# Four stages of the first attention, one turn later in every engine's order

## The chip, the cores and the metric

One core of a Trainium2 chip runs the whole program. Its five engines (TensorE, VectorE, ScalarE, GpSimd and SyncE, in the profile PE, DVE, ACT, POOL and SP) each work through a queue of instructions in order, and wait for one another by semaphores. The metric is the device time of one execution in microseconds, as the median of several runs.

## What is computed

The reference is a block of two layers over `x`, 32 batches of 128 rows and 128 features, with a context of 77 keys per batch. Cut to what matters:

```
x = x + tanh(g_xattn[0]) * attention_0(layernorm(x), ctx)     # one head, masked softmax, layernorm of its result
x = x + tanh(g_ffn[0])   * ffn_0(layernorm(x))                # best of 8 experts by a router, plus a shared expert
x = x + tanh(g_xattn[1]) * attention_1(layernorm(x), ctx)     # 16 heads, relative bias
x = x + tanh(g_ffn[1])   * ffn_1(layernorm(x))                # best of 8 maps by a signature
```

Only the first line and the routing of the second concern the change. The router needs, for each row of the normalised `x`, eight logits (`x_ @ router.T`), the expert of the largest, and then a place for the row among all rows of that expert.

## The kernel before

**The first attention** (`attend_0`) works on pairs of batches, 0 to 15. For a pair, the steps run through four engines:

- TensorE transposes the rows (`rows_T`, L494), multiplies context by weights (`keys`, L509 to L516, and `values`, L502), makes the scores (`scores`, L525), transposes the probabilities (`probs_T`, L533) and weighs the values (`weigh`, L541).
- VectorE makes the bias of the mask (`mask_bias`, L713), the masked scores and their maximum (`masked`, L745, L749), the values with their bias (`values_0`, L723), the statistics of the result (`attend_stats`, L758 to L764), and the new rows with their statistics (`centred` L772, `residual` L784 to L795).
- GpSimd turns variances into factors (`inv_std0`, L892 to L894; `inv_std1`, L902 to L905).
- ScalarE copies results out of PSUM (`keys`, `rows_T`, `probs_T`, `values_1` L641), takes the exponentials (`exps`, L649) and writes the normalised rows `XN` (`norm1`, L660).

**The four stages that the title means** come behind these. TensorE transposes the normalised rows of a pair (`norm1_T`, L549), ScalarE copies the transpose into `XNT` (`norm1_T`, L667), TensorE multiplies it by the router (`logits`, L569). Four pairs make a quarter. When the last pair of a quarter (3, 7, 11, 15) has its logits, VectorE picks the experts and counts them (`route`, L805 to L816), TensorE adds up ranks (`ranks`, L554 and L555), and VectorE turns them into slots (`slots`, L823 to L827). GpSimd then scatters the rows of a batch to their slots in memory (`scatter`, L848): twelve batches within the loop, twenty behind it.

**The order** is written out by hand, for each engine apart. `written_out` takes a list of stages with a lag each; in turn t it issues, in the order of the list, stage by stage, the item t minus its lag (lags count from the smallest in the list). So a stage with a larger lag stands in a later turn, behind the younger pairs' other work. An engine's queue is in order: an instruction that waits holds back all that stand behind it.

Some waits name other pairs than their own, because two stages share a bank of PSUM. `norm1_T` on TensorE (L547) waits until ScalarE has copied the rows' transposes that were issued before it; `norm1_T` on ScalarE (L666) waits for TensorE in the same way; `ranks` (L560) and `scores` (L521) keep the ranks and the scores of one bank apart.

Near the end of the stage, where less work is left per turn, the table also issues filler matmuls (`warm`, L590), whose results nobody reads: in front of the transposes of pairs 14 and 15, behind `weigh` of pair 15, and in front of the logits of pairs 13 to 15.

**What follows.** TensorE ends the stage with the counts (L603) and the ranks of the last quarter. Then the shared expert runs over all rows (`hidden`, L993 and L994; `down`, L1004), while GpSimd issues the remaining scatters. When all scatters have landed and a table of experts is ready, SyncE loads sorted tiles of 128 rows (`xs`, L970), and TensorE transposes them (L1024) and runs the experts. The second attention (`attend_1`) and the second feed-forward take the rest of the program.

Of the kernel before, what the change touches and what calls it, by code (L numbers as in the profile page):

```python
# [47 lines left out]
PAIR = 2  # L48
NG = B // PAIR
QB = 8  # L50
# [85 lines left out]
def wait(eng, sem, value):  # L136

    if isinstance(value, int) and value <= 0:
        return
    eng.wait_ge(sem, value)  # L140
# [27 lines left out]
def written_out(n, stages):  # L168

    first = min(lag for _, lag in stages)  # L170
    for turn in range(n + max(lag for _, lag in stages) - first):
        for stage, lag in stages:
            item = turn - (lag - first)
            if 0 <= item < n:
                stage(item)
# [200 lines left out]
def attend_0(nc, sb, sem, sems, bank, a, m, f, units):  # L376
# [18 lines left out]
    xT = [halves(units["hT"][0][u], 0) for u in two]  # L395
    sm = [sb(f"sm{u}", [128, PAIR, SK]) for u in two]
# [25 lines left out]
    s = sems("a", "w0 cen pe0 act0 stat var rs q xT xTs v v0 v1 mkr mk mb sc sm mx ex pT pTs u umv "  # L422
                  "iv inv z zg xmv inv1 xn1 xT2 xT2s lg sh cum rk wh slot")
# [54 lines left out]
    def pe_program(pe):  # L478
# [39 lines left out]

        def scores(g):
            wait(pe, s["sm"], g)  # L520
            wait(pe, s["wh"], 2 * ((g - 11) // (QB // PAIR)) + 1)  # L521
            pe.wait_ge(s["xTs"], g + 1)
            pe.wait_ge(s["mk"], g + 1)
            for b in range(PAIR):
                last = nc.tensor.matmul(bSC[:, b * SK:(b + 1) * SK], xT[g % 2][:, b, :], M[g % 2][:, b * SK:(b + 1) * SK],  # L525
                                        start=True, stop=True)
            last.then_inc(s["sc"], 1)
# [16 lines left out]
        def norm1_T(g):  # L544
            pe.wait_ge(s["xn1"], g + 1)
            wait(pe, s["xT2s"], g)
            pe.wait_ge(s["xTs"], min(g + 6, NG))  # L547
            for b in range(PAIR):
                last = nc.tensor.transpose(bT2[:, b * 128:b * 128 + 128], XN[:, PAIR * g + b, 0:D], ident)  # L549
            last.then_inc(s["xT2"], 1)  # L550

        def ranked(q):
            pe.wait_ge(s["cum"], q + 1)
            nc.tensor.matmul(place(q), ones[:, :], upto[q % 2][:, :, 1:QB + 1], start=True, stop=False)  # L554
            nc.tensor.matmul(place(q), tri, QH[q % 2][:, :, 1:QB + 1], start=False, stop=True).then_inc(s["rk"], 1)  # L555

        def ranks(g):
            q, i = divmod(g, QB // PAIR)
            if i == QB // PAIR - 1 and q < NQ - 1:
                wait(pe, s["sm"], min(g + 7, NG))  # L560
                if q == NQ - 2:
                    pe.wait_ge(s["mk"], NG)
                ranked(q)
# [23 lines left out]
        def warm(n):  # L587
            pe.wait_ge(s["v1"], NG)
            for k in range(n):
                nc.tensor.matmul(bV[:, 0:3 * PK], identb[:, :], mb[0][:, :, :].rearrange("p (o b) k -> p o (b k)", o=1)  # L590
                                 .to_broadcast([128, 3, PK]), start=True, stop=True)

        def before(table):
            def stage(g):
                if g in table:
                    warm(table[g])
            return stage

        written_out(NG, [(before({14: 7, 15: 3}), 7), (norm1_T, 7), (rows_T, 1), (values, 3), (weigh, 4), (before({15: 6}), 4),
                         (keys, 0), (probs_T, 3), (ranks, 8), (scores, 1), (before({13: 2, 14: 2, 15: 2}), 7), (logits, 7), (unit, 18)])  # L600
        warm(8)
        pe.wait_ge(s["cum"], NQ)
        nc.tensor.matmul(bLG[:, 0:E], ones[:, :], upto[(NQ - 1) % 2][:, :, QB], start=True, stop=True).then_inc(f["s_count"], 1)  # L603
# [2 lines left out]
    def act_program(act):  # L606
# [56 lines left out]

        def norm1_T(g):
            act.wait_ge(s["xT2"], g + 1)
            act.wait_ge(s["xT"], min(g + 7, NG))  # L666
            nc.scalar.activation(XNT[:, pair(g), :], bT2[:, 0:PAIR * S].rearrange("p (b s) -> p b s", b=PAIR),  # L667
                                 ACT.Copy).then_inc(s["xT2s"], 1)

        def unit(j):  # L670
            if j < EARLY:
                for k in range(HC):
                    units["silu"](act, j, k)

        written_out(NG, [(unit, 19), (values_1, 3), (norm1, 6), (probs_T, 3), (keys, 0), (exps, 2), (rows_T, 0), (norm1_T, 6)])

    def dve_program(dve):
        nc.vector.memset(ones[:, :], 1.0).then_inc(s["cen"], 1)
# [158 lines left out]
            if 0 < j <= EARLY:  # L837
                units["add"](dve, j - 1)

        written_out(NG, [(route, 10), (values_0, 5), (attend_stats, 6), (shifted, 5), (centred, 6), (residual, 7), (masked, 3), (slots, 10), (mask_bias, 0), (unit, 20)])  # L840
        dve.wait_ge(s["act0"], 6)
        nc.vector.tensor_scalar(qscale[:, :], qscale[:, :], 4.0, HD ** -0.5, ALU.min, ALU.mult).then_inc(s["cen"], 1)
        dve.wait_ge(s["cen"], 6)
# [904 lines left out]
```

## Time and profile before

| what | value |
|---|---|
| median of 3 runs | 523.37 us (522.79, 523.37, 527.62) |
| the profiled execution | 525.38 us |
| its span, first to last instruction | 523.6 us |
| mean granted clock of TensorE | 0.965 of full speed |
| first attention, shared expert, experts, second layer | to about 108, 140, 222 and 523.6 us |

The profile is of one execution. A line such as L549 is a line of the kernel. In a timeline a row can stand for several instructions of one form that follow each other, and `[0.45 <-ACT XN L660]` says that the engine sat idle for 0.45 us in front of it, until that instruction of ScalarE had ended. Transposes and products of TensorE in this data type are each recorded as two matmuls, so a pair's two transposes are a row of four, two of which overlap their neighbours. "PEclk" is the clock of TensorE that was granted, as a share of its full speed. Times of single rows are of this one execution.

### The profile page before, as it was taken

What the parts mean: (1) busy time and instruction counts of PE and PEld (TensorE: products, weight loads), DVE (VectorE), ACT (ScalarE), POOL (GpSimd) and SP (SyncE); (2) the same over time, 40 slices, a digit from 0 to 9 for tenths busy, and PEclk for the clock granted to TensorE, in tenths of its full rate; (3) what the DMA queues carried; (4) which work ended last, traced back from release to release, by engine and by line L of the source; (5) the groups of instructions that cost most, each with busy time, mean ns of one, the idle gap of its engine ahead of it and who ended that gap; (6) DMA issues with size and microseconds to landing.
All of it is one profiled execution on the core that took longest, in us unless ns stands there. A gap on an engine that the chain in (4) does not pass through costs nothing.

```text
span 523.6 us, 12435 instructions
## 1 busy us (share of the span) xinstructions
PE 482.2 (92%) x3408; PEld 303.7 (58%) x3408; DVE 386.9 (74%) x1178; ACT 300.5 (57%) x981; POOL 346.6 (66%) x813
## 2 busy tenths in 40 slices
PE   6977888799999999879999999999999999999993
PEld 5967776455655666655555555555555555555441
DVE  2879998667333334345899999999999999999852
ACT  3746665322254555266776776676766767776630
POOL 5554777777244555462778787888878787878532
PEclk9979897899999999987999999999999999999997
DMA  8885350022144322100000000000000000000000
GB/s 233 161 113 157 92 160 12 16 77 62 45 106 120 82 74 68 47 11 7 11 13 22 21 12 21 13 21 11 22 13 21 16 19 21 13 17 10 7 6 16
DMA packets 33924, 25.77 MB, mean 49 GB/s; under 512 B 8105, under 2 KB 31281, under 8 KB 33825
## 3 DMA queue, kind: packets, MB, share of 16 engines
q1 hardware_dynamic: 30864, 19.48, 15.3%
q0 software_dynamic: 2272, 4.67, 2.8%
q10 hardware_dynamic: 720, 0.83, 0.6%
q8 instruction: 29, 0.48, 0.4%
q14 instruction: 39, 0.31, 0.2%
HBM read 16.89 MB, written 8.39 MB: 48 GB/s over the span
## 4 chain that ended last, share of the span: by engine, by line
PE 48%; DVE 2%; issue 1%; POOL 1%; POOLq 0%; ACT 0%; DVEq 0%
PE bank L1376 13%; PE bank L1325 8%; PE bank L1311 8%; PE bank L1301 6%; PE bank L1392 2%; PE bank L1362 2%; PE bank L1297 2%; PE bank L1358 1%; PE bank L1342 1%; PE bank L1346 1%; PE bank L1337 1%; PE bank L1287 1%; PE bank L1381 1%; PE bank L1283 1%; PE bank L1398 1%
## 5 line engine op out<-in xcount | busy, mean ns | idle before, releaser
L1439 ACT ACTIVATE wgu<-wgu,top 128x77 f32<-128x77 f32 x256 | 67.4, 347 | 15.7 <-DVE top L1541 15.7
L1376 PE MATMUL bank<-w,xn3T 128*128 128x512 f32 x128 | 71.7, 644 | 0.1
L1449 ACT ACTIVATE PRT<-bank 128x512 f32<-128x512 f32 (+1 forms) x128 | 54.5, 426 | 29.0 <-PE bank L1311 28.5
L983 POOL DMA_INDIRECT routed<-ys,to x39 | 37.4, 960 | 43.7 <-DVE ys L1186 35.0
L1311 PE MATMUL bank<-cst,wgu 128*128 128x128 f32 x320 | 60.2, 286 | 1.6 <-ACT wgu L1439 1.3
L1531 DVE TENSOR_TENSOR wgu<-bank,biasQ 128x616 f32<-128x616 f32 x64 | 50.9, 795 | 7.0 <-PE bank L1301 5.6
L1325 PE MATMUL bank<-PRT,VP 128*32 128x128 f32 x1024 | 55.0, 287 | 0.7 <-ACT PRT L1449 0.7
L1541 DVE TENSOR_REDUCE top<-wgu 128x8 f32<-128x616 f32 x64 | 50.2, 784 | 1.1
L1301 PE MATMUL bank<-KB,QT 32*128 32x308 f32 x256 | 50.2, 433 | 0.0
L1181 DVE TENSOR_TENSOR hid<-actg,bank 128x256 f32<-128x256 f32 x39 | 16.4, 421 | 41.8 <-ACT actg L1090 41.8
L1311 PEld LDWEIGHTS bank<-cst,wgu 128*128 128x128 f32 x320 | 37.7, 142 | 16.1 <-issue 13.2
L1677 POOL TENSOR_TENSOR wgu<-V 128x256 f32<-128x256 f32 x32 | 37.9, 1183 | 6.5 <-DVE V L1602 6.5
L1039 PE MATMUL bank<-wgu,xsT 128*128 x78 | 40.9, 605 | 0.0
L848 POOL DMA_INDIRECT sorted_x<-XN,slot x32 | 33.8, 1056 | 8.5 <-issue 8.5
L1637 POOL TENSOR_TENSOR VP<-XN,cst 128x64 f32<-128x64 f32 x128 | 34.9, 305 | 0.0
L1325 PEld LDWEIGHTS bank<-PRT,VP 128*32 128x32 f32 x1024 | 20.2, 108 | 25.2 <-issue 19.7
L1656 POOL TENSOR_TENSOR x2b<-x,rows 128x128 f32<-128x128 f32 x32 | 14.6, 455 | 27.7 <-DVE x L1569 27.7
L1548 DVE TENSOR_TENSOR wgu<-wgu,top 128x616 f32<-128x616 f32 x32 | 27.1, 846 | 0.0
L1432 ACT ACTIVATE QT<-bank,qbias,qscale 128x128 f32<-128x128 f32 x32 | 14.6, 456 | 21.7 <-PE bank L1287 21.7
L1376 PEld LDWEIGHTS bank<-w,xn3T 128*128 128x128 f32 x128 | 19.1, 188 | 13.4 <-ACT OHT L1482 6.9
L1055 PE MATMUL bank<-wdn,hidT 128*128 x156 | 25.8, 288 | 1.1 <-ACT hidT L1095 1.1
L1090 ACT ACTIVATE actg<-bank 128x256 f32<-128x256 f32 x39 | 15.0, 385 | 19.8 <-PE bank L1039 19.8
(232 smaller groups left out, 1261.6 us busy)
## 6 DMA issues: line engine op xcount, KB each, us to landing
xs<-sorted_x SPq DMA_DIRECT2D x39, 64.5 KB, 1.8
wgu<-in_wgu SPq DMA_DIRECT2D x4, 512.0 KB
y<-routed SPq DMA_DIRECT2D x32, 64.0 KB, 1.8
out<-res SPq DMA_DIRECT2D x32, 64.0 KB, 1.7
ctxT<-in_ctxT SPq DMA_DIRECT2D x16, 77.0 KB, 3.0
mask<-in_mask SPq DMA_DIRECT2D x16, 77.0 KB, 3.8
wdn<-in_wdn SPq DMA_DIRECT2D x2, 512.0 KB
X<-in_x SPq DMA_DIRECT2D x1, 768.0 KB, 5.5
```

Source lines behind the costliest of these rows:

```text
L983: nc.gpsimd.indirect_dma_start(routed, bass.IndirectOffsetOnAxis(ap=to[:, t:t + 1], axis=0), ys[t % WAYS][:, :], None).then_inc(st_y[t % W ...
L1039: nc.tensor.matmul(bH[t % 2][:, :], xsT[t % 2][:, :], wgu[:, bass.ds(experts[t], 1), :], start=True, stop=True).then_inc(e["h"], 1)
L1301: nc.tensor.matmul(bS[i][:, 0:HG * SK], QT[u][rows, :], KB[u][rows, :, :], start=False, stop=True).then_inc(s["sc"], 1)
L1311: last = nc.tensor.transpose(bP[end][:, i * 128:i * 128 + 128], SB[u][:, c, :], ident)
L1325: last = nc.tensor.matmul(bO[32 * j:32 * j + 32, half * S:half * S + S], VP[u][:, half, j, end, :, :].rearrange("p t r -> p (t r)"), PT[ha ...
L1376: nc.tensor.matmul(map_bank(b, k)[:, :], xn3T[u][:, :], w2[:, k * HT:(k + 1) * HT, :], start=True, stop=True).then_inc(s["f"], 1)
L1439: last = nc.scalar.activation(SC[u][:, head, :], SC[u][:, head, :], ACT.Exp, bias=top[u][:, head:head + 1])
L1449: nc.scalar.activation(PT[half][:, k], bP[end][:, 0:k.stop - k.start], ACT.Exp if half else ACT.Copy).then_inc(s["pTs"], 1)
L1531: nc.vector.tensor_tensor(half(SC[u][:, k, :]), bSS.rearrange("p c (h k) -> p c h k", h=HG), half(biasQ[:, k, :]), ALU.add).then_inc(s["sb ...
L1541: nc.vector.tensor_reduce(top[u][:, k], SC[u][:, k, :], AX.X, ALU.max, negate=(h == 0)).then_inc(s["mx" if h else "lo"], 1)
L1637: last = nc.gpsimd.tensor_tensor(VP[u][:, c, :, end, :, 0:HD], VF[:, first:first + HG, bass.ds(b, 1), :].to_broadcast([128, HG, 2, HD]), o ...
L1677: nc.gpsimd.tensor_tensor(sum2[u][:, :, :], picked[u][:, 0:2, :], picked[u][:, 2:4, :], ALU.add).then_inc(s["s2"], 1)
```

## The change

In each engine's list the stages `norm1_T`, `logits`, `route`, `ranks` and `slots` get a lag larger by one: on TensorE `norm1_T` and `logits` 7 becomes 8 and `ranks` 8 becomes 9, with the two fillers' tables that belong to them; on ScalarE `norm1_T` 6 becomes 7; on VectorE `route` and `slots` 10 becomes 11. The waits that count the other pairs between are set to match. `norm1` (L660), GpSimd's and SyncE's lists and all other stages stay. No instruction is added or removed.

```diff
         def scores(g):
             wait(pe, s["sm"], g)
-            wait(pe, s["wh"], 2 * ((g - 11) // (QB // PAIR)) + 1)
+            wait(pe, s["wh"], 2 * ((g - 12) // (QB // PAIR)) + 1)
...
         def norm1_T(g):
             pe.wait_ge(s["xn1"], g + 1)
             wait(pe, s["xT2s"], g)
-            pe.wait_ge(s["xTs"], min(g + 6, NG))
+            pe.wait_ge(s["xTs"], min(g + 7, NG))
...
             if i == QB // PAIR - 1 and q < NQ - 1:
-                wait(pe, s["sm"], min(g + 7, NG))
+                wait(pe, s["sm"], min(g + 8, NG))
...
-        written_out(NG, [(before({14: 7, 15: 3}), 7), (norm1_T, 7), (rows_T, 1), (values, 3), (weigh, 4), (before({15: 6}), 4),
-                         (keys, 0), (probs_T, 3), (ranks, 8), (scores, 1), (before({13: 2, 14: 2, 15: 2}), 7), (logits, 7), (unit, 18)])
+        written_out(NG, [(before({14: 7, 15: 3}), 8), (norm1_T, 8), (rows_T, 1), (values, 3), (weigh, 4), (before({15: 6}), 4),
+                         (keys, 0), (probs_T, 3), (ranks, 9), (scores, 1), (before({13: 2, 14: 2, 15: 2}), 8), (logits, 8), (unit, 18)])
...
         def norm1_T(g):
             act.wait_ge(s["xT2"], g + 1)
-            act.wait_ge(s["xT"], min(g + 7, NG))
+            act.wait_ge(s["xT"], min(g + 8, NG))
...
-        written_out(NG, [(unit, 19), (values_1, 3), (norm1, 6), (probs_T, 3), (keys, 0), (exps, 2), (rows_T, 0), (norm1_T, 6)])
+        written_out(NG, [(unit, 19), (values_1, 3), (norm1, 6), (probs_T, 3), (keys, 0), (exps, 2), (rows_T, 0), (norm1_T, 7)])
...
-        written_out(NG, [(route, 10), (values_0, 5), (attend_stats, 6), (shifted, 5), (centred, 6), (residual, 7), (masked, 3), (slots, 10), (mask_bias, 0), (unit, 20)])
+        written_out(NG, [(route, 11), (values_0, 5), (attend_stats, 6), (shifted, 5), (centred, 6), (residual, 7), (masked, 3), (slots, 11), (mask_bias, 0), (unit, 20)])
```

In the three pieces below, rows without a sign stand in both kernels, rows with - only in the kernel before, rows with + only in the changed one.

ScalarE at the end of its list (`XN` is L660 of a pair, `XNT` the copy of a transpose, L667; the last pair's L660 is the second row):

```order
 L667 ACTIVATE XNT<-bank 128x256
 L660 ACTIVATE XN<-X,nb11,r11 128x128 x2
-L667 ACTIVATE XNT<-bank 128x256
+L667 ACTIVATE XNT<-bank 128x256 x2
 L1074 ACTIVATE wc<-wc 128x8
 L1080 ACT_TABLE_LOAD
```

Before, one copy followed the last L660; now two do, the copy of pair 14 among them.

VectorE behind the residual of pair 13 (L833 is a scaling of weights; the added rows are the statistics of pair 15 and the residual of pair 14; L805 and L806 begin the routing of pair 11):

```order
 L795 BN_AGGR mv<-st 128x2 x2
 L833 TENSOR_SCALAR wc<-wc,tg 128x256
+L758 BN_STATS st<-bank 128x6 x2
+L760 TENSOR_SCALAR es<-bank 128x2
+L764 BN_AGGR mv<-st 128x2 x2
+L772 SCALAR_TENSOR_TENSOR sg<-bank,mv,rows 128x128 x2
+L784 SCALAR_TENSOR_TENSOR X<-sg,ru,X 128x128 x2
+L790 BN_STATS st<-X 128x6 x2
+L795 BN_AGGR mv<-st 128x2 x2
 L805 TENSOR_REDUCE best<-bank 128x8
 L806 TENSOR_TENSOR cand<-bank,best 128x64
```

The routing of pair 11 now stands behind these seven steps; before, they followed it, with the slots of pair 11 between the residuals of pairs 14 and 15.

TensorE behind the weighing of pair 15 (L590 are fillers, L569 the logits of pair 11, L549 the transposes of pair 12, L554 and L555 the ranks of pair 11's quarter):

```order
 L541 MATMUL bank<-V,hT 128x129 x2
 L590 MATMUL bank<-mb,identb 128x462 x6
+L569 MATMUL bank<-wb,XNT 128x8 x2
+L549 MATMUL bank<-cst,XN 128x128 x2
 L554 MATMUL bank<-upto,ones 128x64
 L555 MATMUL bank<-QH,cst 128x64
```

Logits 11 and transposes 12 stood ahead of the weighing and now stand between the fillers and the ranks. What follows the ranks on TensorE (logits 12, transposes 13 and so on, with the fillers) stands in the same order as before.

## Rows read from the trace of the kernel before

**Rows 1.** Page of the profile, part 1: busy us (share of the span) xinstructions, whole span.
```profile
PE 482.2 (92%) x3408; PEld 303.7 (58%) x3408; DVE 386.9 (74%) x1178; ACT 300.5 (57%) x981; POOL 346.6 (66%) x813
```

**Rows 2.** Waits, 36.2 to 85.9 us: who waited for whom: us in total, times, longest us.
```profile
PE bank L549 <- ACT XN L660: 7.6, 8, 2.8
...
DVE mb L713 <- DMA mask<-in_mask: 3.0, 1, 3.0
...
DVE mv L795 <- issue: 0.2, 1, 0.2
```

**Rows 3.** Busy time of VectorE, 36.13 to 85.93 us: us of stretch, busy (instructions), clock, DMA.
```profile
36.13:85.93 49.80, 46.29 (x220) 0.95 0.40 117
```

**Rows 4.** Timeline, one turn: start us, us, engine line operation out<-in [idle before <-releaser].
```profile
40.43 0.23 DVE L713 TENSOR_SCALAR mb<-mask 128x154 bf16<-128x154 int32 x1
...
42.28 0.44 PE L549 MATMUL bank<-cst,XN 128*128 128x128 f32 x2 [0.45 <-ACT XN L660]
...
44.71 0.23 DVE L713 TENSOR_SCALAR mb<-mask 128x154 bf16<-128x154 int32 x1
```

**Rows 5.** Timeline of TensorE, 84 to 109 us.
```profile
87.78 0.69 PE L549 MATMUL bank<-cst,XN 128*128 128x128 f32 x2 [0.91 <-ACT XN L660]
...
96.21 0.41 PE L554 MATMUL bank<-upto,ones 128*128 128x64 f32 x2 [2.09 <-DVE upto L816]
...
98.86 2.78 PE L590 MATMUL bank<-mb,identb 128*128 128x462 bf16 x7
101.48 0.38 PE L549 MATMUL bank<-cst,XN 128*128 128x128 f32 x2
...
102.33 0.61 PE L569 MATMUL bank<-wb,XNT 128*128 128x8 f32 x4
102.80 0.75 PE L590 MATMUL bank<-mb,identb 128*128 128x462 bf16 x3
104.00 0.44 PE L549 MATMUL bank<-cst,XN 128*128 128x128 f32 x2 [0.46 <-ACT XN L660]
...
108.06 1.08 PE L993 MATMUL bank<-XNT,wc 128*128 128x512 f32 x2
```

**Rows 6.** Timeline of VectorE, GpSimd and ScalarE, 89 to 104 us.
```profile
90.21 0.42 DVE L723 TENSOR_TENSOR V<-bank,rows 77x256 f32<-77x256 f32 x1 [0.68 <-PE bank L502]
...
91.07 0.49 DVE L758 BATCH_NORM_STATS2 st<-bank 128x6 f32<-128x128 f32 x2 [0.44 <-PE bank L541]
...
94.36 0.22 DVE L805 TENSOR_REDUCE best<-bank 128x8 f32<-128x64 f32 x1
...
95.98 0.47 DVE L758 BATCH_NORM_STATS2 st<-bank 128x6 f32<-128x128 f32 x2
...
98.82 0.19 DVE L823 TENSOR_TENSOR where<-bank,QH 128x64 f32<-128x64 f32 x1
...
99.53 0.61 DVE L784 SCALAR_TENSOR_TENSOR X<-sg,ru,X 128x128 f32<-128x128 f32 x2
...
101.61 0.21 POOL L902 TENSOR_TENSOR ve<-mv,eps 128x2 f32<-128x2 f32 x1
...
103.07 0.88 ACT L660 ACTIVATE XN<-X,nb,r 128x128 f32<-128x128 f32 x2 [0.79 <-POOL nb L905]
```

**Rows 7.** Granted clock in stretches of the end: TensorE busy (instructions), PEclk, DMA, GB/s.
```profile
98.00:100.00 2.00, 2.00 (x8) 0.51 0.00 0
...
102.00:104.00 2.00, 1.47 (x9) 1.00 0.10 33
```

**Rows 8.** Timeline, 130 to 141 us: the start of the experts.
```profile
134.60 0.96 POOL L848 DMA_INDIRECT sorted_x<-XN,slot  x1 [0.31 <-issue]
...
137.71 2.58 SPq L970 DMA_DIRECT2D xs<-sorted_x  x3
...
140.64 0.33 PE L1024 MATMUL bank<-cst,xs 128*128 128x128 f32 x1 [0.33 <-DMA xs<-sorted_x]
```

**Rows 9.** Busy time, 108.06 to 140.2 us: PE, PEld, DVE, ACT, POOL, PEclk, DMA, GB/s.
```profile
108.06:140.20 32.14, 32.05 (x149) 20.13 (x148) 21.44 (x53) 7.17 (x12) 21.43 (x20) 1.00 0.24 65
```

## The prediction

> **What bounds the kernel now.** I read the page first, then the waits of the first attention, then one turn of the timeline, then its end engine by engine. The page shows TensorE busy for 92% of the span and VectorE for 74% [rows 1]; over the whole program TensorE is the engine to relieve. The stretch that the change touches is different, so the share of the span decides nothing here.
>
> In the waits of 36.2 to 85.9 us TensorE stands 7.6 us in front of L549, the transposes of the normalised rows, for ScalarE's L660 [rows 2]. That is the wait which the change addresses. The same view has only two entries for VectorE: one load of a mask, 3.0 us, which ends where the stretch begins (what TensorE lost or wins ahead of it is swallowed by that load), and 0.2 us without a releaser. VectorE waits for no other engine in these 50 us. It is busy for 46.29 of 49.80 us; the rest lies between instructions of its own chain [rows 3]. One turn shows the same: two L713 of neighbouring turns start 4.28 us apart, and inside that turn TensorE idles 0.45 us in front of L549 [rows 4]. So VectorE sets the turn from 36 to 86 us, and what TensorE waits there is slack.
>
> The end is another matter. At 90.21 and 91.07 VectorE does wait for TensorE, 0.68 and 0.44 us, for L502 and L541 [rows 6], which stand behind L549 at 87.78, itself 0.91 us late for L660 [rows 5]. From there a chain leads to the next stage: statistics of the last pair on VectorE, L902 and its followers on GpSimd (101.61), L660 on ScalarE (103.07), L549 (104.00), the logits L569 of that pair, the last routing on VectorE, and L993 at 108.06 [rows 5, 6]. From 108.06 TensorE works through the shared feed-forward without a gap, 32.05 of 32.14 us [rows 9]. Beside it GpSimd issues one scatter after another, the last at 134.60, the loads of sorted rows start at 137.71, and the second tile's transpose waits 0.33 us for its load at 140.64 [rows 8]. Two chains thus end within a microsecond of each other at 140: a gain in one alone is worth little.
>
> **The change part by part.** No instruction is added or removed and no DMA moves; GpSimd and SyncE keep their order. The summed durations stay; only positions in three queues count.
>
> *The turns from 36 to 86 us: 0.* TensorE's 7.6 us of waiting for L660 go, because the transposes of a pair stand a turn (4.28 us) behind it. What is late next is VectorE itself: L502 needs the bank that L723 and L641 free, and these follow VectorE's turn. The routing of pairs 3 and 7 and their slots come a turn later. By the rows of pair 11 that is 1.62 us (L805 at 94.36 to L758 at 95.98) and 0.71 us (L823 at 98.82 to L784 at 99.53) [rows 6]; they move within VectorE's continuous work and change no total. The scatters wait for the slots; the first is the only one near its limit, and GpSimd is busy with the statistics of that turn until about the time the slots are ready, so I add 0. Bounds: a gain of at most the 7.6 us if I misread VectorE, a loss of some 5 us if each of twelve turns lost as much as one L549 wait (0.45 us). I take 0, the row nearest being VectorE's own two entries.
>
> *The end on VectorE: a gain of 1.8 us.* L502 no longer waits behind L549, so the 0.68 and 0.44 us go: 1.12. The slots of pair 11 (0.71 us) now stand behind the residual of the last pair, not ahead of it. The routing of pair 11 moves from ahead of the statistics of pair 15 to behind the residual of pair 14, but it is still ahead of the last residual, so its 1.62 us neither come back nor are added. Together 1.8. GpSimd's own queue allows slightly less: between two statistics stands one scatter of about 1.3 us (0.96 and 0.31 in front of it at 134.60 [rows 8]), so I expect L902 of the last pair about 1.6 us earlier, near 100.0 instead of 101.61, and L660's pair ending near 102.3 instead of 103.95 (103.07 + 0.88).
>
> *The end on TensorE and ScalarE: a loss of 1.5 to 4.5 us on the same chain.* ScalarE's copy of a transpose (L667) now stands behind the L660 of the next pair. So the copy for pair 14 cannot start before L660 of pair 15 has ended, and on TensorE the logits of pair 14, three filler matmuls, and only then the transpose of pair 15 follow. Before, these lay in the time in which L660 of pair 15 was awaited: logits 14 at 102.33, fillers at 102.80, 0.75 long, and the transpose at 104.00 directly behind L660 [rows 5]. Now they stand behind it: copy 0.4 (the later half of the 0.85 us from transpose 14 at 101.48 to logits 14 at 102.33), logits 0.47 (102.33 to 102.80), fillers about 0.65 (0.75 with the last one's tail): 1.5 to 1.6 us at the full clock. From 102.3 this gives the transpose of pair 15 at 103.85, against 104.00: the gain of 1.6 is used up, net -0.1.
>
> The price at the lower clock is the open term. TensorE idles 2.09 us in front of L554 at 96.21, and between 98 and 100 us the granted clock is 0.51, its lower level of 1.2 GHz; there seven fillers take 2.78 us, 98.86 to 101.48 [rows 5, 7]. Three at 102.80, where the clock is full again (1.00 over 102 to 104), take 0.75, so seven would take about 1.5 there. In the changed order L554 waits for a routing that stands behind 2.84 us more of VectorE's work (L758 at 95.98 to L823 at 98.82), less the 1.1 gained before: 1.7 us later, and ahead of L554 TensorE now has logits 11 and transposes 12 as well, under 1 us. I estimate an idle time of 2.5 us or more. If the low level then covers logits 13 and the seven fillers, transpose 14 comes near 102.8 and that of pair 15 near 104.7: net +0.7. If it covers the whole end, every step doubles: logits and fillers 2.2 for 1.1, the seven fillers 2.6 for 1.5, transposes and the rank matmuls another 0.8: net +2.9. So the term lies between -0.1 and +2.9, and I take +0.7, the case nearest to the rows of before, where the low level covered 98 to 100 and was over by 102 [rows 7].
> The Trainium skill, page "TensorE: Matmul & The Clock Gate", Part 1 on the HAM clock gate, says that the throttled state is the default and that activity releases it, so an engine that has idled starts slow; it speaks against this change, because the idle time ahead of L554 grows. The rows at 96.21 and 98 to 100 us agree with it: idle, then the lower level. By the rule the sum is the +0.7 or the +2.9; by the full clock alone it would be -0.1.
>
> *The start of the experts: -0.3 us.* The scatters end about 1.6 us earlier, so the load for the second tile is there in time: the 0.33 us at 140.64 go [rows 8]. No more, since later loads wait for buffers that TensorE frees.
>
> **The sum.** 0 (turns) + 0.7 (end, net) - 0.3 (experts) = +0.4 us, against 525.38 us of the profiled execution (span 523.6, and 1.8 around it): 525.8. The median of the runs, 523.37, lies 2.0 below that execution; the same difference on it gives 523.8 us. About 1%, or 5.2 us, is what a measurement of this kernel can tell from no change.
>
> **The rivals.**
> A. *The end runs at the lower clock throughout*: +2.9 - 0.3, 526.0 us, slower. For it: the longer idle time in front of L554 and filler matmuls that stand on the path. Against it: in the rows of before the low level was over by 102. It decides from the point where transpose 14 comes after 103.
> B. *The gain of the end stays*: ScalarE's copy is early enough, and GpSimd's scatters set the start of the experts: -1.6 us, 521.8. For it: two chains of nearly equal length at 140. Against it: L667 of pair 14 stands behind L660 of pair 15 in ScalarE's queue, which is in order.
> C. *TensorE's wait was on the path*: the 7.6 us of the turns and the 0.91 and 0.46 us of the end come back, 9.0 us: 514.4 us. For it: TensorE's 92%. Against it: VectorE's two entries.
> D. *VectorE's turns get waits that they had not*: the transposes now follow the logits of an older pair, and if VectorE lost 0.45 us in each of twelve turns, +5.4: 529 us. For it: nothing in the rows but the tight order of ScalarE, in which L660 is not moved. Against it: TensorE gets slack, not work.
>
> **Chances.** The forecast 0.57 (522.3 to 525.3 by itself), A 0.20, B 0.12, C 0.06, D 0.05. The range: A and B lie inside a range of 521.0 to 527.0, C and D outside, 11 in 100; with the spread of single runs (522.79 to 527.62) I keep 520.8 to 527.2. Faster by over 1%: C, and a little of B with luck, 0.07. Slower by over 1%: D and what A may add where the low level reaches into the shared feed-forward, 0.05. Within 1%: 0.88.
>
> **What would show it.** Right: the 7.6 us in front of L549 gone or below 1 us; neighbouring L713 still 4.28 us apart; VectorE still without waits from 36 to 86 us; the wait at 90 us gone, L660 of pair 15 ending about 1.6 us earlier, but L549 of pair 15 no longer directly behind it: logits 14 and fillers between; L993 within a microsecond of 108. Wrong: a turn below 4.2 us (C), new waits of VectorE (D), L993 at 106.5 with scatters as the last thing awaited (B), or at 111 with a clock of 0.5 from 98 on (A).

## The result, and the profile after

| kernel | median | against before | 95% interval |
|---|---|---|---|
| before, 20 executions beside it | 523.56 us | 1 | |
| after, 20 executions | 526.87 us (523.35 to 532.36) | 1.0059 | 1.0042 to 1.0075 |

The change costs 3.3 us by the medians, 0.6%: inside the range of 520.8 to 527.2, and 3.1 us above the forecast of 523.8. This is less than the 1% that the prediction took for the least to be told from no change, but the interval leaves no change out. All ratios here leave out executions that stood far off the others of their kernel.

The profiled execution of after took 525.73 us (span 523.9), no longer than that of before. That likeness misleads. The last mask load that VectorE waits for (L713, at the start of the turns) came at 36.13 us in before and at 33.29 in after; over all profiles of this study it came between 33.31 and 36.13 where the turns stand as in before, and between 31.93 and 33.98 where they stand as in after. The load was issued at 25.51 and 21.89 us, ahead of the first instruction that the change moves (L549, at 30.58 in before). So the change did not bring these 2.84 us: after had luck there. I measure from that load to L993, the start of the shared expert:

| stretch | before | after | difference |
|---|---|---|---|
| last mask to L805, the routing of pair 11 | 36.13 to 94.36: 58.23 | 33.29 to 94.45: 61.16 | +2.93 |
| L805 to L554, the ranks of pair 11 | to 96.21: 1.85 | to 96.34: 1.89 | +0.04 |
| L554 to L993 | to 108.06: 11.85 | to 108.29: 11.95 | +0.10 |
| last mask to L993 | 71.93 | 75.00 | +3.07 |

Behind L993 these two profiles show no difference: 523.6 - 108.06 = 415.5 us and 523.9 - 108.29 = 415.6. Nearly the whole difference (2.93 of 3.07) is there when VectorE starts to route pair 11.

**The turns.** The waits of after over the same length from its own mask load, 33.4 to 83.1 us (who waited for whom: us in total, times, longest):

```profile
PE bank L502 <- ACT V L641: 2.3, 2, 2.1
PE bank L554 <- DVE upto L816: 2.2, 1, 2.2
PE bank L541 <- ACT hT L655: 1.7, 2, 1.4
DVE mb L713 <- DMA mask<-in_mask: 1.6, 1, 1.6
```

and the busy time of VectorE in it (us of stretch, busy, clock, DMA):

```profile
33.29:83.09 49.80, 46.23 (x220) 0.91 0.41 117
```

L549 with its 7.6 us [rows 2] is gone from the list. VectorE did not gain: 46.23 of 49.80 us, against 46.29 [rows 3]. TensorE's waiting time went elsewhere, and into fewer, longer pieces: 2.1 in front of L502, 1.4 in front of L541, 2.2 in front of L554.

**The end.** VectorE of after, 83 to 97 us (start, length, instruction, idle time ahead of it and its releaser):

```profile
83.27 0.42 DVE L723 TENSOR_TENSOR V<-bank,rows 77x256 f32<-77x256 f32 x1 [0.36 <-PE bank L502]
84.13 0.49 DVE L758 BATCH_NORM_STATS2 st<-bank 128x6 f32<-128x128 f32 x2 [0.44 <-PE bank L541]
87.43 0.42 DVE L723 TENSOR_TENSOR V<-bank,rows 77x256 f32<-77x256 f32 x1 [0.17 <-PE bank L502]
88.29 0.49 DVE L758 BATCH_NORM_STATS2 st<-bank 128x6 f32<-128x128 f32 x2 [0.44 <-PE bank L541]
...
91.58 0.49 DVE L758 BATCH_NORM_STATS2 st<-bank 128x6 f32<-128x128 f32 x2
92.98 0.61 DVE L784 SCALAR_TENSOR_TENSOR X<-sg,ru,X 128x128 f32<-128x128 f32 x2
94.45 0.19 DVE L805 TENSOR_REDUCE best<-bank 128x8 f32<-128x64 f32 x1
96.11 0.59 DVE L784 SCALAR_TENSOR_TENSOR X<-sg,ru,X 128x128 f32<-128x128 f32 x2
```

The two waits of [rows 6], 0.68 and 0.44, became four, 1.41 in sum. The routing (94.45) stands behind the statistics of pair 15 and the residual of pair 14: 94.45 - 91.58 = 2.87 us of work that it used to precede. TensorE, and below it ScalarE, at the same end (the row by itself is L603 of before):

```profile
78.30 0.66 PE L554 MATMUL bank<-upto,ones 128*128 128x64 f32 x2 [2.20 <-DVE upto L816]
...
96.34 0.66 PE L554 MATMUL bank<-upto,ones 128*128 128x64 f32 x2 [3.87 <-DVE upto L816]
...
100.05 2.50 PE L590 MATMUL bank<-mb,identb 128*128 128x462 bf16 x7
102.39 0.38 PE L549 MATMUL bank<-cst,XN 128*128 128x128 f32 x2
...
103.71 0.74 PE L590 MATMUL bank<-mb,identb 128*128 128x462 bf16 x3
104.29 0.38 PE L549 MATMUL bank<-cst,XN 128*128 128x128 f32 x2
...
107.57 0.39 PE L603 MATMUL bank<-upto,ones 128*128 128x8 f32 x2 [0.24 <-DVE upto L816]
...
108.29 1.08 PE L993 MATMUL bank<-XNT,wc 128*128 128x512 f32 x2
```

```profile
107.34 0.39 PE L603 MATMUL bank<-upto,ones 128*128 128x8 f32 x2 [0.23 <-DVE upto L816]
```

```profile
98.74 0.38 ACT L667 ACTIVATE XNT<-bank 128x256 f32<-128x256 f32 x1 [0.87 <-PE bank L549]
99.64 0.88 ACT L660 ACTIVATE XN<-X,nb,r 128x128 f32<-128x128 f32 x2 [0.52 <-POOL nb L905]
102.80 0.38 ACT L667 ACTIVATE XNT<-bank 128x256 f32<-128x256 f32 x1 [2.29 <-PE bank L549]
```

The last L660 ends at 100.52, and the last transposes start at 104.29, 3.77 us later, with no wait in front of them. In [rows 5, 6] they started 0.05 us behind it (104.00 against 103.95). So XN of pair 15 is no longer what the end waits for; from L554 to L993 TensorE has only one wait left, 0.24 us ahead of L603. ScalarE's copy for pair 14 waited 2.29 us for TensorE, not TensorE for it.

**The clock.** TensorE in four stretches of after, and in the first two of before (busy, clock, DMA, GB/s):

```profile
79.00:88.00 9.00, 9.00 (x36) 0.50 0.05 17
95.50:102.00 6.50, 5.66 (x22) 0.50 0.06 20
98.00:100.00 2.00, 2.00 (x9) 0.50 0.10 33
102.00:104.00 2.00, 1.92 (x13) 0.99 0.17 58
```

```profile
79.00:88.00 9.00, 6.53 (x38) 0.80 0.02 8
95.50:102.00 6.50, 5.70 (x27) 0.74 0.03 11
```

Behind both long waits for the routing the lower level (1.2 GHz) stands longer than in this profile of before; it is over by 102, as in [rows 7]. At the end this alone does not make the 3 us: in the second profile of before (next section) the lower level stands there as long as in after.

### The profile page after: what moved, and what is told of

It reads as the page before. It is cut to its first block, busy times and chain, and to the rows that moved or that the text cites. A ratio compares the mean times of both kernels' runs of the same rounds, so it can differ in the third digit from the quotient of the medians.

```text
span 523.9 us, 12434 instructions
## 1 busy us (share of the span) xinstructions
PE 483.0 (92%) x3408; PEld 303.2 (58%) x3408; DVE 386.2 (74%) x1178; ACT 300.2 (57%) x981; POOL 345.8 (66%) x813
## 4 chain that ended last, share of the span: by engine, by line
PE 48%; DVE 2%; issue 1%; POOL 1%; POOLq 0%; ACT 0%; DVEq 0%
PE bank L1376 13%; PE bank L1325 8%; PE bank L1311 8%; PE bank L1301 6%; PE bank L1392 2%; PE bank L1362 2%; PE bank L1297 2%; PE bank L1358 1%; PE bank L1342 1%; PE bank L1346 1%; PE bank L1337 1%; PE bank L1287 1%; PE bank L1381 1%; PE bank L1283 1%; PE bank L1398 1%
```

## The experiments

A line number in an experiment can stand some lines lower than in before and after (XN is L666 in place of L660, for instance); the text names the step. "The way" is the time from the last mask load to L993, in the one profile of each kernel (in e7 the view puts the start, 33.50, down to TensorE; the load, issued at 22.44, landed 11.0 us later, at the same moment). Each ratio is against executions of before beside that kernel.

| kernel | the way, us | median, us | against before |
|---|---|---|---|
| before; again | 71.93; 72.24 | 523.56; 523.68 | 1; 1.0013 (0.9987 to 1.0038) |
| after; again | 75.00; 75.07 | 526.87; 526.44 | 1.0059; 1.0065 (1.0038 to 1.0092) |
| e4, late turns, early end | 75.27 | 525.07 | 1.0031 (1.0001 to 1.0061) |
| e5, early turns, late end | 74.61 | 524.64 | 1.0038 (1.0014 to 1.0062) |
| e1, after, routing 11 early | 78.11 | 527.44 | 1.0099 (1.0064 to 1.0134) |
| e2, after, fillers out | 74.38 | 524.06 | 1.0029 (1.0002 to 1.0055) |
| e3, before, fillers out | 73.19 | 525.58 | 1.0033 (1.0000 to 1.0067) |
| e6, after, waits filled | 82.20 | two groups | 0.9998 (0.9958 to 1.0038) |
| e7, before, waits filled | 71.91 | 521.01 | 0.9962 (0.9928 to 0.9997) |
| e8, after, ranks 11 late | 75.22 | 527.32 | 1.0082 (1.0053 to 1.0111) |
| e10, e7 with more fills | 72.98 | 523.42 | 0.9983 (0.9958 to 1.0008) |
| e12, e8 and ScalarE's copies early | 72.13 | 524.18 | 1.0023 (0.9996 to 1.0049) |

**Both kernels again.** No edit.

> The kernel before once more, unchanged, for a second profile. Theory 2: the waits stand as in the first (L549 up to 2.8 once, else under 1.3 until 92 us); with about 9 us of low clock between 76 and 108 us, as there, 71.9 us from the last mask to L993, and up to 3 us more where the clock is low for longer. The first mask load may come at another time than 36.13, as it did in all the other profiles (31.9 to 35.2).

> The kernel after once more, unchanged, for a second profile. Theory 2 (the loss comes with the stretches of low granted clock behind TensorE's longest waits): where between 76 and 108 us the clock stands at 0.50 for longer than the 16 us or so of the first profile, the way from the last mask to L993 is longer than 75.0 us, where for less, shorter; the waits themselves (about 2.1 ahead of L502, 1.5 to 2.8 ahead of L541, 2.2 ahead of L554 of pair 7) are there again. Rival (the order alone): 75.0 within 0.5 whatever the clock.

The way came out at 72.24 (34.59 to 106.83) and 75.07 (32.87 to 107.94), with the same waits in after, 2.20 ahead of L554 of pair 7 and 3.86 ahead of that of pair 11, and the low clock again from 78 to 88 and 95 to 101 us. The 3 us are no accident of one profile. In before the mask load and the low stretches moved (one lay at 35 to 42 us), and the way kept its length within 0.3. The expectation of up to 3 us more under a longer low stretch did not come true at the end, where the lower level stood from 93.5 to 100 us, against 98 to 101.5 in the first profile:

```profile
94.00:96.00 2.00, 1.72 (x7) 0.50 0.01 4
96.00:98.00 2.00, 2.00 (x10) 0.50 0.10 33
98.00:100.00 2.00, 2.00 (x9) 0.50 0.00 0
```

In both profiles of after the clock was alike, so they do not part the clock from the order.

**Turns and end apart (e4, e5).**

```diff
+    put_off = lambda g: g < 10            # e5: g >= 10
+    def both(stage, lag):
+        def only(keep):
+            return lambda g: stage(g) if put_off(g) == keep else None
+        return [(only(True), lag + 1), (only(False), lag)]
...
-        written_out(NG, [(route, 11), (values_0, 5),
+        written_out(NG, [*both(route, 10), (values_0, 5),
```

(and so for the other moved stages)

> Pairs 0 to 9 stand one turn later, as in the kernel after; pairs 10 to 15 stand as in the kernel before, so one turn carries pairs 9 and 10 together. Theory 1 (the end alone costs: from the last mask to L993 the kernel after takes 75.00 us against 71.93, +2.97 of it by L554 of pair 11): time as before, 523.6 us within 1, ratio 0.998 to 1.002. Rival (the turns cost: TensorE's new waits of 2.2 ahead of L554 of pair 7 and 2.1 ahead of L502, and the lower clock behind them): as after, 526 to 527 us, ratio 1.004 to 1.007. If the turn that carries two pairs costs by itself, up to 2 us is seen there, around TensorE's L549 of pair 10, and nowhere later.

> The other half: pairs 0 to 9 stand as in the kernel before, pairs 10 to 15 one turn later, as in the kernel after (one turn carries no pair). Theory 1 (the end alone costs): as after, 526.9 us within 1, ratio 1.004 to 1.008, and from the last mask to L993 about 75 us. Rival (the turns cost): as before, 523.6 us within 1, from the last mask to L993 about 72 us.

Neither theory fits: by the time each half costs about half, with intervals that reach up into that of after. In e5 the way is 74.61, near after's, as the end's theory wants. In e4, whose end stands as in before, VectorE lost its time in the turns:

```profile
65.87 0.42 DVE L730 TENSOR_TENSOR V<-bank,rows 77x256 f32<-77x256 f32 x1 [1.24 <-PE bank L509]
66.73 0.49 DVE L765 BATCH_NORM_STATS2 st<-bank 128x6 f32<-128x128 f32 x2 [0.44 <-PE bank L548]
86.97 0.42 DVE L730 TENSOR_TENSOR V<-bank,rows 77x256 f32<-77x256 f32 x1 [1.53 <-PE bank L509]
87.79 0.49 DVE L765 BATCH_NORM_STATS2 st<-bank 128x6 f32<-128x128 f32 x2 [0.40 <-PE bank L548]
```

3.61 us, where before lost 1.12. Ahead of both places the clock was at 0.5 (0.57 over 60 to 62, 0.50 over 82 to 84). The second place says nothing of the order, since it is the turn that carries two pairs, 9 and 10, which the expectation had named. There TensorE makes the transposes of both ahead of L509, 1.19 us apart:

```profile
83.38 0.67 PE L556 MATMUL bank<-cst,XN 128*128 128x128 f32 x2
84.57 0.66 PE L556 MATMUL bank<-cst,XN 128*128 128x128 f32 x2 [0.52 <-issue]
```

The first place, 1.68 us, has the order of after. The same two waits stand in e6 (1.31 and 0.44 us at 65.85 and 66.71, with the clock low from 60 to 67), which has the order of after up to there, and in neither profile of after. So the late order of the turns lost 1.7 us there in two executions and 0.3 or nothing in the others profiled; that the lower clock makes the difference is likely, but no run sets it apart.

**The routing of pair 11 alone (e1).**

```diff
-        written_out(NG, [(route, 11), (values_0, 5), ...
+        written_out(NG, [(only(route, lambda g: g != 11), 11), (only(route, lambda g: g == 11), 10), (values_0, 5), ...
```

> The kernel after with one move undone: VectorE's routing of pair 11 (L805 and what follows it, 2.84 us) stands ahead of the statistics of pair 15 again, as before; everything else stays one turn later. Theory 1 (the place of this routing on VectorE holds L554 on TensorE, and L554 holds all that stands behind it there up to L993): L554's wait of 3.87 falls to 1 or 1.5, L993 comes 2.3 to 2.8 us earlier against the last mask, 524 to 524.6 us, ratio 1.001 to 1.003; XN of pair 15 comes back to its late place and is L549's new wait. Rival (ScalarE's copy L667 of pair 14 behind L660 of pair 15, and the clock after it, are the loss): L993 within 0.7 us of after or later, 526 to 527.5 us.

L554 did come earlier, 62.38 us behind the mask against 63.05, but L993 came 3.1 later: the theory that this one place is the loss falls. VectorE now waited 2.15 us for the logits of pair 11, which stand late on TensorE, and everything behind slid: XN of pair 14 came at 98.74. Then TensorE waited for something new:

```profile
99.94 1.02 PE L569 MATMUL bank<-wb,XNT 128*128 128x8 f32 x4 [3.35 <-ACT XNT L667]
```

```profile
98.74 0.88 ACT L660 ACTIVATE XN<-X,nb,r 128x128 f32<-128x128 f32 x2 [5.64 <-POOL nb L908]
99.53 0.36 ACT L667 ACTIVATE XNT<-bank 128x256 f32<-128x256 f32 x1
```

The copy for pair 13 stood behind XN of pair 14 on ScalarE, and the seven fillers and all else of TensorE's end behind these logits. This is the hold that the prediction had named, one pair earlier than it had put it.

**The fillers (e2, e3).** After and before without 16 of the end's fillers:

```diff
-        written_out(NG, [(before({14: 7, 15: 3}), 8), (norm1_T, 8), ..., (scores, 1), (before({13: 2, 14: 2, 15: 2}), 8), (logits, 8), (unit, 18)])
+        written_out(NG, [(norm1_T, 8), ..., (scores, 1), (logits, 8), (unit, 18)])
```

> The kernel after without 16 of the end's filler matmuls (L590: the 7 and 3 ahead of the transposes of pairs 14 and 15, and the 2, 2, 2 ahead of the logits of pairs 13 to 15); nothing that they compute is read. The 6 and the last 8 stay. Theory 1 (in the kernel after TensorE is behind from L554 on, so its fillers stand on the path: 7 of them took 2.50 us, 2 about 0.5, 3 about 0.5): L993 3 to 4 us earlier against the last mask, about 523.5 us, ratio 0.998 to 1.002. Rival (the fillers stand in time in which TensorE would wait for ScalarE's copies anyway, or the clock stays at its lower level for longer without them): L993 within 1 us of after, 526 to 528 us.

> The kernel before without the same 16 filler matmuls of the end (7, 3, 2, 2, 2); nothing that they compute is read. In before the last transposes waited 0.46 us for XN of pair 15, so the fillers stand in waiting time: Theory 1: -0.4 to +0.5, ratio 0.999 to 1.001, with L549 of pair 15 still behind XN. Rival (they keep the clock up): the clock stays at 0.50 through the end as it did in the kernel after without them (95 to 108 us), and the last logits, L603, L554 and the first of L993 take twice as long: +1.5 to +2.5 us, 525 to 526 us.

Without them after has a way of 74.38, 0.6 shorter, and before one of 73.19, 1.3 longer. In both the clock then stayed at 0.50 from 98 to the end of the stage or nearly so, and the eight fillers that were left took 3.24 us, not 1.72. The last transposes and these fillers in e2:

```profile
101.17 0.67 PE L549 MATMUL bank<-cst,XN 128*128 128x128 f32 x2
...
103.18 3.24 PE L590 MATMUL bank<-mb,identb 128*128 128x462 bf16 x8
```

So in before the fillers stand in waiting time and seem to earn their place by the clock: in e3 it is 5.91 us from the last transposes to L993, in before 4.06; the ratio, 1.0033, has an interval that begins at 1. In after they stand on the path. Without them it is 5.97 us from L554 to the last transposes (95.20 to 101.17) in place of 7.95, but 6.22 from there to L993 in place of 4.00: what they cost, the lower clock took back. The 0.6 us were won ahead of them (L554 at 62.19 behind the mask, in after 63.05).

**The waits for the routing filled (e6, e7).** Matmuls whose result the next matmul overwrites, ahead of the two L554, with (0, 9, 16) of them in after and (0, 5, 9) in before:

```diff
+                for k in range((0, 9, 16)[q]):
+                    nc.tensor.matmul(place(q), tri, tri[:, 0:E * QB].rearrange("p (e b) -> p e b", e=E), start=True, stop=True)
                 ranked(q)
```

> The kernel after, with matmuls whose result is overwritten unread in two of TensorE's own waits: 9 (64 columns, about 0.2 us each at the higher clock) ahead of L554 of pair 7, which waited 2.20 us, and 16 ahead of L554 of pair 11, which waited 3.87. Theory 2 (behind each of these two waits the granted clock stood at 0.50: from 79 to 88 us, which made VectorE wait 1.41 us, and from 95.5 to 102 us, where it doubled what TensorE does between L554 and L993): with TensorE busy the clock stays at 1.00 there, VectorE's waits go (-1.4) and the way from L554 to L993 falls from 11.95 to 9 or 10 us (-2 to -3): 522.5 to 524 us, ratio 0.998 to 1.002. Rival (the order of instructions alone is the loss, the clock falls anyway): 526 to 527.5 us, ratio 1.005 or more.

> The kernel before with the same kind of matmuls in the same two waits, fewer since the waits are shorter: 5 ahead of L554 of pair 7 (waited 1.24), 9 ahead of L554 of pair 11 (waited 2.09). Theory 2: the clock's fall at 98 to 101 us goes, but the end of before ran at ScalarE's L660 of pair 15 (103.07), which TensorE's clock doesn't move: -0.7 to 0, 522.8 to 523.5 us. Rival (TensorE's clock bounds the end of before too): -1.5 to -2, 521.5 to 522 us. If the added matmuls run over the end of a wait: up to +1.

After with fills ran in two groups: six of twelve executions took 520.94 to 523.01 us, 4 to 6 under the median of after, three 528.04 to 528.29, and three more than that. The profile is of the execution of 528.29:

```profile
86.63 1.24 PE L502 MATMUL bank<-wb,ctxT 128*77 128x256 f32 x4 [1.97 <-ACT V L643]
...
96.36 6.93 PE L564 MATMUL bank<-cst 128*128 128x64 f32 x32
```

```profile
102.00:104.00 2.00, 2.00 (x12) 0.50 0.10 33
```

Behind pair 7 the fills kept the clock at 1.00 until 86 us. Then came the next long wait, 1.97 ahead of L502, the clock fell, and the 16 fills took 6.93 us where the wait was 3.9. That the faster executions were faster because the clock stood is possible, but none of them was profiled. In before the fills brought -0.4%, with an interval that ends just under 1; e7 is the only kernel here whose interval lies below 1. The way is 71.91, as in before, so its gain is not where I expected it, and where it lies is open.

**More fills (e10).** The kernel of e7, with fills ahead of six of the L549:

```diff
+            for k in range({4: 10, 5: 3, 7: 2, 10: 3, 11: 2, 14: 5}.get(g, 0)):
+                nc.tensor.matmul(bT2[:, 0:64], tri, tri[:, 0:64], start=True, stop=True)
             pe.wait_ge(s["xn1"], g + 1)
```

> The kernel before with the fills of e7 (5 and 9 ahead of the two L554) and more of them (0.24 us each) ahead of the transposes L549 that waited for XN: 10 for pair 4 (waited 2.77), 3, 2, 3, 2 and 5 for pairs 5, 7, 10, 11 and 14 (waited 0.97, 0.80, 0.99, 0.81, 1.43 in the profile of e7). Theory 2 (the low clock from 50 to 54 and from 81 to 88 us, which made VectorE wait 0.67 and 0.44, stands behind these waits): these stretches go, 1.1 us less than e7 from the last mask to L993 (70.8 against 71.9): 520 us, ratio 0.992 to 0.996. Rival (the clock falls there anyway, and the added matmuls then run over the end of the waits): 521 to 523 us, ratio 0.996 to 1.000, with the added matmuls at 0.45 us each in a low stretch.

A miss. The low stretch of 81 to 88 us was gone, and another came at 57 to 61 and at 91 to 95, where L549 had waited 1.97 and the fills ahead of L554 took 2.77 us for 2.12. The low stretches behind 50 us came to 7 us, in e7 to some 10, and the way was 1.1 us longer all the same: fewer of them did not make it shorter.

**Ranks of pair 11 late on TensorE (e8), and ScalarE's copies early as well (e12).**

```diff
-    logit = bLG[:, 0:QB * E]...
+    logit = lambda q: (bSC if q == NQ - 1 else bLG)[:, 0:QB * E]...
...
+            if q == NQ - 1 and i == 0:
+                pe.wait_ge(s["sm"], NG)
+                pe.wait_ge(s["wh"], 2 * (NQ - 2))
...
-  (ranks, 9), ..., (logits, 8), (unit, 18)])
+  (only(ranks, lambda g: g != 11), 9), ..., (logits, 8), (only(ranks, lambda g: g == 11), 11), (unit, 18)])
...                                        # e12, on ScalarE
-  (norm1, 6), ..., (norm1_T, 7)])
+  (only(norm1_T, lambda g: g >= 12), 7), (norm1, 6), ..., (only(norm1_T, lambda g: g < 12), 7)])
```

> The kernel after with the logits of pairs 12 to 15 in another bank than those of pairs 8 to 11, so that they need not wait until VectorE has read these, and TensorE's L554 of pair 11 behind the logits of pair 14. Theory 1b (in the kernel after everything on TensorE from the logits of pair 12 on stands behind L554 and so behind VectorE's routing of pair 11, at 96.34, though XN of pair 13 was there at 93.83): the wait of 3.87 goes to waits for XN, the last transposes follow XN of pair 15 (100.52) by less than 1 us instead of 3.8, L993 3 to 4 us earlier: 522.5 to 523.5 us, ratio 0.996 to 1.000. Rival (TensorE's low clock and its fillers bound the end wherever L554 stands): L993 at most 1 us earlier, 525.5 to 527 us.

> The kernel of e8 (logits of pairs 12 to 15 in another bank, L554 of pair 11 behind the logits of pair 14) with one more move: on ScalarE the copies L667 of pairs 12 to 15 stand ahead of XN (L660) of the next pair, as in the kernel before, not behind it. Theory 3 (in the kernel after two holds stand within 2 us of each other, the routing of pair 11 ahead of L554 and ScalarE's copy of pair 13 behind XN of pair 14; taking one away, in e1 and e8, only shows the other: the logits of pair 13 waited 3.35 and 2.49 for the copy there): the logits of pair 13 start 2 us earlier than in e8, the last transposes follow XN of pair 15 by less than 1 us (4.0 in e8), L993 comes 71 to 72.5 us behind the last mask (75.2 in e8, 75.0 in after): 522.5 to 524.5 us, ratio 0.998 to 1.002. Rival (TensorE's low clock and the fillers fill the time anyway): L993 74 us or more behind the mask, 525.5 to 527.5 us.

In e8 the wait of 3.87 was gone and nothing was gained. TensorE and ScalarE of e8:

```profile
95.55 0.41 PE L549 MATMUL bank<-cst,XN 128*128 128x128 f32 x2
95.81 0.55 PE L596 MATMUL bank<-mb,identb 128*128 128x462 bf16 x2
98.85 1.02 PE L572 MATMUL bank<-wb,XNT 128*128 128x8 f32 x4 [2.49 <-ACT XNT L673]
```

```profile
97.66 0.88 ACT L666 ACTIVATE XN<-X,nb,r 128x128 f32<-128x128 f32 x2 [2.62 <-POOL nb L911]
98.44 0.36 ACT L673 ACTIVATE XNT<-bank 128x256 f32<-128x256 f32 x1
```

The transposes of pair 13 were done by 96, their copy came at 98.44 behind XN of pair 14, and the logits waited 2.49 us: the second hold, as in e1. With the copies ahead of it, in e12:

```profile
94.36 0.38 ACT L673 ACTIVATE XNT<-bank 128x256 f32<-128x256 f32 x1 [0.53 <-PE bank L549]
95.81 0.88 ACT L666 ACTIVATE XN<-X,nb,r 128x128 f32<-128x128 f32 x2 [1.06 <-POOL nb L915]
...
98.99 0.87 ACT L666 ACTIVATE XN<-X,nb,r 128x128 f32<-128x128 f32 x2
```

```profile
94.80 0.84 PE L572 MATMUL bank<-wb,XNT 128*128 128x8 f32 x4
...
100.67 0.38 PE L549 MATMUL bank<-cst,XN 128*128 128x128 f32 x2
...
104.67 1.08 PE L1003 MATMUL bank<-XNT,wc 128*128 128x512 f32 x2
```

The logits of pair 13 start at 94.80, the last transposes 0.8 us behind the end of the last XN (98.99 + 0.87), where e8 has 4.0 and after 3.8, and the way is 104.67 - 32.54 = 72.13: 3.1 less than in e8 and 0.2 from before, though the clock stood at 0.50 from 78 to 91 us, longer than in after. The last XN itself ends no earlier than in after (67.32 and 67.23 us behind the mask), so the gain lies in the holds. The time follows, 1.0023 against 1.0082, but less sharply than the way: the profile is of the fastest execution (519.90; the others took 521.72 to 526.69), the interval reaches up to 1.0049, and e2, with both holds, stands at 1.0029. So in the way the loss of the end is the two holds together. The first hides the second, and taking the first away alone (e1, e8) gains nothing. The second alone was not taken away; in after ScalarE's copy for pair 13 waited 0.87 us for TensorE (98.74, above), so there it does not hold anything.

## Why the prediction came out as it did

*The turns, 0*: right for after, in both its profiles. L549's waits went, VectorE's busy share did not change, a turn is 4.3 us still (33.29 to 37.59 and 41.87 for the next L713). Rival C, which made TensorE's waits the bound, is ruled out. The price that I bounded by 0.45 a turn appeared in another form: not in each turn but behind one long wait, as VectorE's four waits from 83 to 88 us (in e4 and e6 1.7 us at another place).

*The end on VectorE, a gain of 1.8*: too large by 1.2. XN of pair 15 starts 66.35 us behind the mask (99.64 - 33.29) against 66.94: 0.6 earlier, not 1.6. The 0.71 of the slots was there. The 1.12 of the two waits was not: I had laid them to L549 and XN, but TensorE now came late to L502 and L541 of other turns, with the low clock from 79 to 88 us, and VectorE waited 1.41.

*The end on TensorE and ScalarE, net +0.7 within -0.1 to +2.9*: this is the step that failed, measured at +3.07. I let the chain begin at the last L660 and asked what stands behind it. I had worked out that L554 would come late (I wrote 1.7 us; it was 2.97), but used this only to judge the clock. The chain begins there. Of the +2.93 that VectorE's routing is late, 2.87 is the work that it now stands behind, 0.29 the longer waits, and -0.23 remains. Behind L554 TensorE of before had waits of 0.46 [rows 5] and 0.23 us in all, and more than that a late L554 could not use up. The 0.23, ahead of L603, is still there in after (0.24), because that wait is for the last routing and moves with the rest. The 0.46 is gone, and the lower clock took it back: from L554 to the transposes of pair 14 it was 5.27 us in before (96.21 to 101.48) and 6.05 in after (96.34 to 102.39). I could have read that. My own 1.7 us, put on 101.48, give 103.2 for these transposes, where I wrote 102.8.

That the time still lies inside the range is luck as far as this step goes: the end measured more than its own upper bound of +2.9, and the range went up to 527.2 for the spread of single runs, not for a mechanism (A, the highest inside it, gave 526.0).

ScalarE's copy behind the next XN was the right hold at the wrong pair: it binds pair 13, not 14, and in after it lies hidden behind L554 (e1, e8). With both gone the way comes back to 72.13 (e12).

*The start of the experts, -0.3*: right in kind. L1024 waits for nothing at 140.27, 31.98 us behind L993 (32.58 before), but later loads take that back (from 140 to 222 us TensorE waits 4.3 us for them, in before 2.8): nothing of it is left in the 415.6 us.

*The rivals.* A has the nearest time, 526.0, and not its mechanism: it was to decide if transposes 14 came after 103, and they came at 102.39, with the clock at 0.99 from 102. B fell because the scatters' lead (the last one issued at 131.04, in before at 134.60) was worth nothing with TensorE as the later chain. D is true in part, with 0.3 us more of waits in place of 5.4.

The clock: after a long idle time ahead of L554 the granted clock fell to its lower level in both profiles of after, at 78 and at 95 us, and stayed there for some 10 and 7 us. Not every such wait does this: in e5 TensorE waited 2.76 us up to 50.42 and 2.08 up to 84.44, and the clock stood at 1.00 from 49 to 56 and from 84 to 88. The Trainium skill, page "TensorE: Matmul & The Clock Gate", Part 1 on the HAM clock gate, says that the throttled state is the default and that activity releases it. The first half agrees with the rows of after. Against the second half stand rows in which work went on and the clock did not rise: in after TensorE was busy for 9.00 of 9.00 us from 79 to 88, all at 0.50, and in e6 without a gap from 93 to 110.

## What to carry to other kernels

When a step is moved later in one engine's order, look up who waits for it, and add up the waits that stand behind that waiter in its own queue: that sum is the most that it can hide (here 0.7 us against 2.9). Idle time that is taken from one place of a queue can come back at another: the change removed 7.6 us of waits, seven of eight of them under 1 us, and waits of 2.1, 2.2 and 3.9 us came in their place, each with a stretch of the lower clock behind it. And a hold that shows no wait may lie behind another one; if undoing one part of a change gives nothing, undo two.

## What was not expected

Profiles differ by up to 4 us in when one small load lands (31.93 to 36.13 us for the last mask; 34.59 and 36.13 in the two of before), so spans of single profiles say little here; a stretch measured from that load repeated within 0.3 us. The part behind L993 varied from 410.5 us (e6, 526.5 - 116.05) to 416.9 (e8, 526.1 - 109.20) with no edit in it, and by 1.2 us between the two profiles of after (415.6 and 416.8); this is open, and it is why a way and a median can differ by a microsecond or more. And a busy TensorE did not bring its clock back for 17 us in e6 (93 to 110), with 32 small matmuls, the logits and the fillers following without a gap.
